# A transformer layer on one Trainium2 core: value norms moved into the output weights, four attention output buffers, spread normalisations and no paired units

## The reference

```python
def _L0_attn_ref(x, wq, wk, wv, wo, q_norm_w, k_norm_w):
    xq = _rms_norm(x @ wq.T, q_norm_w, EPS)      # 32 heads of 64
    xk = _rms_norm(x @ wk.T, k_norm_w, EPS)      # 8 heads of 64
    xv = x @ wv.T
    ...
    allowed = (dist <= 0) & (dist >= -SLIDING_WINDOW)     # 256
    bias = jnp.where(allowed[None], alibi, -jnp.inf)
    scores = jnp.einsum('bhtd,bhsd->bhts', xq, xk) * scale + bias[None]
    attn = jax.nn.softmax(scores, axis=-1)
    out = jnp.einsum('bhts,bhsd->bhtd', attn, xv)
    out = out.transpose(0, 2, 1, 3).reshape(bsz, seqlen, N_HEADS * HEAD_DIM)
    return out @ wo.T
...
x = x + _layernorm(_L0_attn_ref(_layernorm(x), ...))
x = x + _layernorm(_L0_ffn_ref(_layernorm(x), ...))   # silu(x Wg * gs) * (x Wu * us) Wd * ds, 1408 wide
```

## Time and profile before

| | |
|---|---|
| median of 3 runs | 1206.97 us (1206.37 to 1208.41) |
| the profiled execution | 1207.18 us, span 1205.0 us |
| granted TensorE clock, mean | 0.994 |
| PE busy | 1164.7 us (97% of the span) |
| DVE busy | 891.2 us (74%) |
| ACT busy | 745.9 us (62%) |
| POOL busy | 392.1 us (33%) |

### The profile page before, as it was taken

One profiled execution on the slowest core, in us unless ns is written; L12 is line 12 of the kernel. 1 busy time (PEld: TensorE's weight loads), 2 busy tenths in 40 slices (PEclk: granted clock), 3 DMA queues, 4 the chain that ended last, 5 costly groups with the idle time before them and its releaser, 6 DMA issues.

```text
span 1205.0 us, 26933 instructions
## 1 busy us (share of the span) xinstructions
PE 1164.7 (97%) x9016; PEld 994.3 (83%) x9016; DVE 891.2 (74%) x2328; ACT 745.9 (62%) x1582; POOL 392.1 (33%) x465
## 2 busy tenths in 40 slices
PE   7999999999888899999999999999999999999997
PEld 5878888887777788898989898898888888888876
DVE  5587778687888878888888888888866575546464
ACT  4646555555888778888878888788862443222230
POOL 3000000001799865354544545354531100202022
PEclk9999999999999999999999999999999999999999
DMA  5216355347667774556545664556437440303020
GB/s 175 105 45 245 141 212 206 140 193 261 215 232 246 245 252 137 184 164 220 158 152 178 205 203 139 179 171 217 128 95 237 146 130 30 105 1 106 1 70 36
DMA packets 100132, 189.89 MB, mean 158 GB/s; under 512 B 8352, under 2 KB 38176, under 8 KB 100000
## 3 DMA queue, kind: packets, MB, share of 16 engines
q1 hardware_dynamic: 100000, 188.21, 46.3%
HBM read 116.54 MB, written 71.63 MB: 156 GB/s over the span
## 4 chain that ended last, share of the span: by engine, by line
PE 88%; POOL 5%; DVE 3%; issue 2%; ACT 1%; DMA 1%; SPq 0%; POOLq 0%; DVEq 0%; ACTq 0%
PE bank L1384 21%; PE bank L1517 19%; PE bank L1449 15%; PE bank L1322 11%; PE bank L1410 10%; PE bank L1428 2%; PE bank L1438 2%; PE bank L1426 2%; PE bank L1427 2%; POOL qk L697 1%; POOL bias L663 1%; POOL o_mid L672 1%; DMA q_st<-q_scr 1%; POOL o_out L678 1%; PE bank L1494 1%
## 5 line engine op out<-in xcount | busy, mean ns | idle before, releaser
L781 ACT ACTIVATE p_sb<-u_sb,low 128x384 f32<-128x384 f32 (+2 forms) x512 | 272.5, 536 | 49.4 <-DVE low L1030 40.8
L1030 DVE CUSTOM_DVE_ANT_0 u_sb<-bank,bias 128x384 f32<-128x384 f32 (+2 forms) x512 | 229.8, 452 | 50.8 <-PE bank L1322 28.2
L1322 PE MATMUL bank<-k_st,q_st 128*128 128x384 f32 (+2 forms) x1024 | 254.7, 331 | 1.9 <-DMA q_st<-q_scr 1.4
L1410 PE MATMUL bank<-ident,p_sb 128*128 128x128 f32 x1152 | 218.3, 280 | 21.0 <-ACT p_sb L781 13.7
L1144 DVE TENSOR_TENSOR pT_lo<-bank,pT_hi 128x384 f16<-128x384 f32 (+2 forms) x392 | 178.5, 455 | 34.5 <-ACT pT_hi L889 27.4
L889 ACT ACTIVATE pT_hi<-bank 128x384 f16<-128x384 f32 (+2 forms) x392 | 159.9, 408 | 42.9 <-PE bank L1410 38.3
L1322 PEld LDWEIGHTS bank<-k_st,q_st 128*128 128x128 f32 x1024 | 170.5, 193 | 18.9 <-DMA q_st<-q_scr 1.7
L1410 PEld LDWEIGHTS bank<-ident,p_sb 128*128 128x128 f32 x1152 | 141.1, 141 | 51.3 <-ACT p_sb L781 27.9
L672 POOL TENSOR_TENSOR o_mid<-o_raw,inv_sum 128x256 f32<-128x256 f32 x128 | 83.8, 654 | 227.8 <-DVE inv_sum L1156 226.3
L634 POOL TENSOR_TENSOR rstd<-var_eps,minus_half 128x1 f32<-128x1 f32 (+1 forms) x30 | 22.6, 752 | 413.8 <-DVE var_eps L999 413.8
L1517 PE MATMUL bank<-zT_hi,gu 128*128 128x512 f32 x352 | 139.3, 396 | 0.6 <-DVE hid L1273 0.6
(11 more groups left out here) (128 smaller groups left out, 2396.1 us busy)
## 6 DMA issues: line engine op xcount, KB each, us to landing
q_scr<-qk SPq DMA_DIRECT2D x64, 512.0 KB, 2.7
q_st<-q_scr SPq DMA_DIRECT2D x32, 1024.0 KB, 7.8
k_st<-k_scr SPq DMA_DIRECT2D x64, 256.0 KB, 3.2
o_scr<-o_out SPq DMA_DIRECT2D x128, 128.0 KB, 2.9
o_in<-o_scr SPq DMA_DIRECT2D x16, 768.0 KB, 5.2
k_scr<-qk SPq DMA_DIRECT2D x16, 512.0 KB, 2.6
z_in<-z_scr SPq DMA_DIRECT2D x8, 1024.0 KB, 5.9
v_scr<-v_out SPq DMA_DIRECT2D x4, 1040.0 KB, 6.6
```

The source lines that it names most:

```text
L781: nc.scalar.activation(p_sb[:, u % RING, 0:w], u_sb[:, u % RING, 0:w], ACT.Exp, scale=-1.0, bias=low[:, u % RING:u % RING + 1]).then_inc(p ...
L1030: nc.vector.tensor_tensor_reduce(out=u_sb[:, u % RING, 0:w], in0=bank[u % 2][:, 0:w], in1=bias[2 * u // UNITS][:, u % REP, at:at + w], sca ...
L1322: mm = nc.tensor.matmul(bank[u % 2][:, 0:w], q_st[:, s, r, P * i:P * i + P], k_st[:, s, part, P * key:P * key + w], start=(part == 0), sto ...
L1410: mm = nc.tensor.transpose(bank[probability_bank(A)][:, P * j:P * j + P], p_sb[:, u % RING, P * j:P * j + P], ident[:])
```

## The change

- The norms of the values go into wo: `split_wo` first multiplies a chunk of wo by `vn_col`, which holds the norms of two heads as a column (row d of wo belongs to value dimension d), then rounds and subtracts as before. `vn_col` is loaded from one row of `vn_scr` by two transfers of 512 elements of 4 bytes. `finish_o` is one multiplication.
- `o_raw` and `inv_sum` have four buffers (`O_RING`), released by `o_ready`.
- Late normalisations: four in group 0, three in groups 1 and 2, none in 3, and one each in groups 4 to 10, at unit 8. The last seven chunks (f = 13 to 19) have memory of their own (`raw_last`) and one buffer of their own (`qk_late`). SP checks the ring's stores in group 3 (`rings_stored`).
- TWINS = 0: each unit is rounded and split by itself from the start, by `LAGS`, through banks 2 and 3.

```diff
-TWINS = LAG * UNITS - 2 * TT
+TWINS = 0
 RING = 4
+O_RING = TT
...
-LATE_UNITS = (2, 4, 18, 20, 22)
+LATE_COUNTS = {0: 4, 1: 3, 2: 3, **{n: 1 for n in range(LAG, LAG + 7)}}
+LATE_AT = {4: (2, 4, 18, 20), 3: (4, 18, 20), 1: (8,)}
 LATE_NORMS = {}
-for _k, _f in enumerate(range(LATE, QC + KVC)):
-    LATE_NORMS[_k // len(LATE_UNITS), LATE_UNITS[_k % len(LATE_UNITS)]] = _f
+for _n, _count in LATE_COUNTS.items():
+    for _u in LATE_AT[_count]:
+        LATE_NORMS[_n, _u] = LATE + len(LATE_NORMS)
+LATE_OWN = LATE + sum(_count for _n, _count in LATE_COUNTS.items() if _n < LAG)
...
-            inv_sum = sb(s2, "inv_sum", [P, 2, REP])
-            sb(s2, "spare", [P, REP * HD])
-            o_raw = sb(s2, "o_raw", [P, 2, REP, O_COLS])
-            o_mid = sb(s2, "o_mid", [P, REP, HD])
+            inv_sum = sb(s2, "inv_sum", [P, O_RING, REP])
+            o_raw = sb(s2, "o_raw", [P, O_RING, REP, O_COLS])
...
+        def own(b, f):
+
+            return isinstance(b, int) and b == B - 1 and f >= LATE_OWN
+
+        def qk_buffer(b, f):
+
+            return qk_late if own(b, f) else qk[:, f % QK_RING]
...
+            def rings_stored():
+
+                for s in range(QK_RING):
+                    sp.wait_ge(qk_stored[s], qk_stores(B - 1, 0) + DMA * len(range(s, LATE_OWN, QK_RING)))
+                sp.wait_ge(v_stored, DMA * B)
...
-            sp.dma_start(v_norm[:, 0:G].rearrange("p g d -> p (g d)"), vn_scr).then_inc(vn_loaded, DMA)
-            sp.dma_start(v_norm[:, G:G + 2].rearrange("p g d -> p (g d)"), vn_scr[:, 0:2 * HD]).then_inc(vn_loaded, DMA)
+            for half in range(2):
+                sp.dma_start(vn_col[HD * half:HD * half + HD, :], vn_scr[0].rearrange("(g d) -> d g", g=G),
+                             allow_slow_non_contiguous=True).then_inc(vn_loaded, DMA)
...
                 pool.wait_ge(inv_sum_ready, a + 1)
-                at_least(pool, o_ready, a)
-                nc.gpsimd.tensor_tensor(out=o_mid[:], in0=o_raw[:, i % 2, :, 0:HD],
-                                        in1=inv_sum[:, i % 2].unsqueeze(2).broadcast_to([P, REP, HD]),
-                                        op=ALU.mult).then_inc(o_mid_ready, 1)
-                pool.wait_ge(o_mid_ready, a + 1)
                 at_least(pool, o_stored[i], DMA * (2 * n + s))
                 hold(pool)
-                nc.gpsimd.tensor_tensor(out=o_out[:, i], in0=o_mid[:],
-                                        in1=v_norm[:, 2 * (n % TT) + s:2 * (n % TT) + s + 1].broadcast_to([P, REP, HD]),
+                nc.gpsimd.tensor_tensor(out=o_out[:, i], in0=o_raw[:, i, :, 0:HD],
+                                        in1=inv_sum[:, i].unsqueeze(2).broadcast_to([P, REP, HD]),
                                         op=ALU.mult).then_inc(o_ready, 1)
...
+                chunk = TT * group + i
+                g = 2 * chunk // REP
                 pool.wait_ge(wo_loaded, DMA * (group + 1))
...
+                nc.gpsimd.tensor_tensor(out=wo_stage[:, i], in0=wo_stage[:, i], in1=vn_col[:, g:g + 1].broadcast_to([P, D]),
+                                        op=ALU.mult).then_inc(wo_scaled, 1)
+                pool.wait_ge(wo_scaled, chunk + 1)
+                nc.gpsimd.tensor_copy(wo_hi[:, chunk], wo_stage[:, i]).then_inc(wo_hi_ready, 1)
...
-                at_least(act, o_mid_ready, a - 1)
-                nc.scalar.activation(o_raw[:, u // REP % 2].rearrange("p r d -> p (r d)"),
+                at_least(act, o_ready, a - O_RING + 1)
+                nc.scalar.activation(o_raw[:, u // REP % O_RING].rearrange("p r d -> p (r d)"),
...
                 if A < TWINS:
                     at_least(pe, pT_ready, A - A % 2 - 2)
                 else:
-                    at_least(pe, pT_ready, A - 1 if A > TWINS + 1 else TWINS - 2)
+                    at_least(pe, pT_ready, A - 1)
```

More of the change, by code:

```diff
@@ L126, in feed_forward_slots @@
     return slots
-LATE_UNITS = (2, 4, 18, 20, 22)
+LATE_COUNTS = {0: 4, 1: 3, 2: 3, **{n: 1 for n in range(LAG, LAG + 7)}}
+LATE_AT = {4: (2, 4, 18, 20), 3: (4, 18, 20), 1: (8,)}
 LATE_NORMS = {}
-for _k, _f in enumerate(range(LATE, QC + KVC)):
-    LATE_NORMS[_k // len(LATE_UNITS), LATE_UNITS[_k % len(LATE_UNITS)]] = _f
+for _n, _count in LATE_COUNTS.items():
+    for _u in LATE_AT[_count]:
+        LATE_NORMS[_n, _u] = LATE + len(LATE_NORMS)
+LATE_OWN = LATE + sum(_count for _n, _count in LATE_COUNTS.items() if _n < LAG)
 def late_norms(n, first, end):
-    return [LATE_NORMS[n, u] for u in LATE_UNITS if first <= u < end and (n, u) in LATE_NORMS]
+    return [LATE_NORMS[n, u] for u in range(first, end) if (n, u) in LATE_NORMS]
 SLOTS = feed_forward_slots()
@@ L261, in sandwich_layer @@
             norm_w = sb(s1, "norm_w", [P, QC + KVC])
-            with ExitStack() as before_norms:
-                w_stage = sb(before_norms, "w_stage", [P, 2, KC, T])
-            qk = sb(s1, "qk", [P, QK_RING, 2, T], F32R)
+            inv_rms = sb(s1, "inv_rms", [P, 2, T])
+            raw_last = sb(s1, "raw_last", [P, QC + KVC - LATE_OWN, T])
+            raw = [raw_first[:, f] if f < LATE_OWN else raw_last[:, f - LATE_OWN] for f in range(QC + KVC)]
         with ExitStack() as s2:
@@ L274, in sandwich_layer @@
             y_raw = sb(s2, "y_raw", [P, D])
-            sb(s2, "spare4", [P, REP * WIN - D])
-            v_norm = sb(s2, "v_norm", [P, G + 2, HD])
+            qk_late = sb(s2, "qk_late", [P, 2, T], F32R)
+            vn_col = sb(s2, "vn_col", [P, G])
+            sb(s2, "spare5", [P, (G + 2) * HD - G])
             f_bits = sb(s2, "f_bits", [P, PARTS, D])
@@ L444, in store_qk @@
                 sp.dma_start(scr[bass.ds(head, 2)].rearrange("h d t n -> (h d) t n"),
[L445 removed]
+                             qk_buffer(b, f)[:].bitcast(F32)).then_inc(qk_late_stored if own(b, f) else qk_stored[f % QK_RING], DMA)
             def stage1_stored(batches):
@@ L812, in square_v @@
                 for kc in range(KC):
-                    nc.scalar.activation(raw[:, QC + kc], w_stage[:, 1, kc], ACT.Square).then_inc(v_squared, 1)
+                    nc.scalar.activation(raw[QC + kc], w_stage[:, 1, kc], ACT.Square).then_inc(v_squared, 1)
             def norm_of_v():
                 act.wait_ge(v_norm_psum, 1)
-                nc.scalar.activation(raw[:, QC + KVC - 1], bank[7][:], ACT.Sqrt, scale=VSCALE ** -2,
+                nc.scalar.activation(raw[QC + KVC - 1], bank[7][:], ACT.Sqrt, scale=VSCALE ** -2,
                                      bias=eps_tiny[:]).then_inc(v_norm_ready, 1)
@@ L822, in round_raw @@
                 act.wait_ge(scaled, (QC + KVC) * b + f + 1)
-                at_least(act, qk_stored[f % QK_RING], qk_stores(b, f))
-                nc.scalar.activation(qk[:, f % QK_RING, 0], raw[:, f], ACT.Copy).then_inc(qk_hi_ready, 1)
+                if own(b, f):
+                    at_least(act, qk_late_stored, DMA * (f - LATE_OWN))
+                else:
+                    at_least(act, qk_stored[f % QK_RING], qk_stores(b, f))
+                nc.scalar.activation(qk_buffer(b, f)[:, 0], raw[f], ACT.Copy).then_inc(qk_hi_ready, 1)
             def project(b, last=False):
@@ L851, in project @@
                         at_least(act, qk_ready, (QC + KVC) * (b - 1) + n + 1)
-                        nc.scalar.activation(raw[:, n], bank[n % 4][:], ACT.Copy).then_inc(raw_ready, 1)
+                        nc.scalar.activation(raw[n], bank[n % 4][:], ACT.Copy).then_inc(raw_ready, 1)
                         if n in (0, QC):
@@ L1356, in project @@
                             pe.wait_ge(v_squared, kc + 1)
-                            mm = nc.tensor.matmul(bank[7][:], ones[:], raw[:, QC + kc], start=(kc == 0), stop=(kc == KC - 1))
+                            mm = nc.tensor.matmul(bank[7][:], ones[:], raw[QC + kc], start=(kc == 0), stop=(kc == KC - 1))
                         mm.then_inc(v_norm_psum, 1)
```

39 lines of the change are left out of this document (19 added, 20 removed).

## The result

The changed kernel takes 1216.68 us (median of 4 runs, 1214.99 to 1217.69), the kernel before beside it 1207.69 (median of 4). The ratio is 1.0074, its 95% interval 1.0061 to 1.0087. So it is slower, by 0.7%, as forecast (1210.1), but by 9.0 us instead of 2.9, and 0.7 us above the end of the range. The profiled execution took 1217.23 us with a span of 1215.5, from the first to the last instruction.

What follows compares the result with a forecast made beforehand. PE was taken to bound the attention from group 4 on (99% busy), POOL's stalls to slow groups 0 to 3. Groups 0 to 3 -9.3, unit 8 of groups 4 to 10 +12.2: +2.9 on 1207.2 gives 1210.1 us, range 1201 to 1216.

Steps and rivals of the forecast that it cites:

- (a): Groups 0 to 3: POOL's shorter work and four o_raw buffers remove the stalls, -10.9 us.
- (b): Groups 0 to 3: seven of 17 late normalisations leave, -2.8 us; the ten that stay cost +0.2 each, +2.0.
- the rule: Groups 0 to 3 without stalls: 7.7 us a heavy quarter, 7.1 a light one, 0.4 a late normalisation, 125.9 in all.
- (c): Groups 0 to 3, couples dissolved: heavy quarters +9.6 us, light quarters -7.2, net +2.4.
- Its chain: Single units on ACT and DVE: round, split, add_bias, exp, round; 2.09 us for two units, plus 0.26 for o_raw's copy.
- (e): Groups 4 to 10, unit 8: DVE's scaling waits for POOL's bias, PE stalls; 1.75 us seven times, +12.2.
- (f): Groups 11 to 15, projections and feed forward: only POOL's finish_o gets shorter, 0 us.
- Rival A: Groups 4 to 10: the scaling meets no bias, so unit 8 costs 3.5 us; 1201.4 us, chance 0.33.
- C: Rival, groups 1 to 3: POOL still ends last, only 5 us of stalls go; 1216.0 us, chance 0.09.
- B: Rival, groups 0 to 3: single units take 1.17 us each, light quarters gain nothing; 13.6 us, 1221.3 total, chance 0.10.
- The prediction's own sign of being wrong: Scalings of 0.75 us at unit 8 with groups of 39.3 us, or groups 0 to 3 above 131 us together.

Runs made afterwards that it cites:

- e4: The changed kernel with units below 120 coupled again as in the kernel before; groups 0 to 3 together took 123.7 us.
- e12: The changed kernel with single units below 120 at the couples' lags through four PSUM banks, seven late normalisations at unit 12; 1194.15 us, ratio 0.9889 to before.
- e1: The changed kernel with POOL making only 16 of 384 bias columns for units 16 to 31 in groups 4 to 10; 1209.11 us.
- e2: The changed kernel with the seven late normalisations of groups 4 to 10 at unit 12 instead of 8; 1205.81 us.
- e11: The changed kernel with the seven scalings at unit 8 cut to 16 of 512 columns, POOL's bias whole; groups took 40.3 us.
- e7: The changed kernel with DVE's split four units behind instead of three and weighing five behind, below unit 120; groups 0 to 3 took 160.3 us.
- e8: The kernel before with only the couples dissolved (TWINS = 0); groups 0 to 3 together took 138.6 us.

## Why the prediction was right in sign and too small

- **(a) and (b), stalls and moved normalisations: right.** -10.9 - 2.8 = -13.7 was said; with couples kept, e4 measures 123.7 - 136.8 = -13.2. Some luck is in this: in e4 the eight heavy quarters took 64.5 us where the rule has 61.6, because the last of group 3 takes 9.9 and not 7.7, and the light ones with their ten normalisations and the start 59.1 where it has 61.5. POOL's busy time, 26.4 us in group 1, came below the 28.8 said, of which 1.6 were waits.
- **(c), couples: the step that failed.** +2.4 was said; +4.4 with the +2.0 for the ten that stay, which the prediction has in (b), for POOL's third wo operation. Measured was +9.5 for both. What failed is the gain of the light quarters in single units, and the price of a late normalisation there. Its chain stands: heavy quarters take 8.64 us (8.9 said), and in the kernel after the chain reads as foretold. ACT and DVE of group 1, the units 10 to 13, against the earlier trace rows:

```profile
340.36 0.56 DVE L1168 TENSOR_TENSOR pT_lo<-bank,pT_hi 128x384 f16<-128x384 f32 x1
...
341.43 0.62 ACT L802 ACTIVATE p_sb<-u_sb,low 128x384 f32<-128x384 f32 x1 [0.15 <-DVE low L1054]
341.95 0.37 ACT L925 ACTIVATE o_raw<-bank 128x260 f32<-128x260 f32 x1
342.21 0.48 ACT L913 ACTIVATE pT_hi<-bank 128x384 f16<-128x384 f32 x1
...
342.73 0.56 DVE L1168 TENSOR_TENSOR pT_lo<-bank,pT_hi 128x384 f16<-128x384 f32 x1 [0.20 <-ACT pT_hi L913]
```

  From split to split of one parity 2.37 us with the copy of o_raw in it, where the prediction has 2.09 + 0.26. By its terms, from the starts of the exponentials in e4 and in the kernel after: heavy quarters, said +9.6, measured +6.0 (seven are 0.6 to 1.4 dearer, the last of group 3 is 0.4 cheaper). Light quarters, said -7.2, measured 8 x (6.63 - 6.84) = -1.7: I took 6.2 from a quarter of group 7, where a unit has 1.1 us and the chain is slack, and 7.07, the coupled one, still had 0.2 in it that e4 hasn't. Remaining normalisations, said +2.0, measured +5.2, what is left of the 9.5. One reason was foreseen, the scalings held by POOL (five of them by 0.4 us, so up to 2 us). The other wasn't: DVE's scaling and ACT's copy come into a chain that has little room for them, and I had priced them by what they cost where two units shared an instruction. With the other lags of e12, where no scaling lasts over 0.80 us, one still costs 0.7, (7.60 - 6.2) / 2. How the 5.2 us divide between the two no run tells.
- **(e), the collision: right in mechanism, 1.5 us short.** Said: bias 552.0 to 554.8 beside unit 8, scaling to 0.55 behind it, DVE 1.75 us late, 1.75 us a group, 12.2 in all. Measured: a scaling of 1.82 us that holds DVE for 1.75 (557.00 to 558.75), 2.0 a group, 13.7 in all. Only its parts were mis-sized: I gave 0.65 to a normalisation without collision (0.5 and 0.15 by e), e1 gives 0.97; the bias adds 1.05, not 1.1.
- **(f): right within 0.6 us** of 193.2 for groups 11 to 15.
- Rival A, no collision, is refuted by the seven scalings of 1.73 to 1.83 us. Had the seven stood at unit 12, the same working would have given A's 1201.4; e2 took 1205.81, so (c) would have missed there too. C is refuted by POOL's 79%. B's chain of 1.17 us a unit is refuted by heavy quarters of 8.64 (1.08 a unit), but its other half, no gain in light quarters, was nearly what came. The prediction's own sign of being wrong, groups 0 to 3 above 131 us, came as well (133.1).
- By the profiles the sum was 10.5 us, 1.4 of them ahead of the attention; by the medians 9.0. Against the forecast (c) with the +2.0 gave 5.1 more, (e) 1.5, (a) and (b) 0.5, and groups 11 to 15 with what follows 0.9 less: 2.9 + 6.2 = 9.1.

## What to carry to other kernels

Before a VectorE instruction with two operands in SBUF is moved, look up on POOL's time line what runs at the new place: a collision costs what is left of POOL's instruction, even for a moved one of sixteen columns (e11), and costs it on the path if the stretch has no slack. And a construct that comes as a bundle (two units an instruction, other lags, more banks) should be taken apart before it is judged: here the lags with the banks were worth 11 us, and the four groups were 1.8 us shorter without the pairing. A chain is read by writing down which instruction stands ahead of which on each engine, and counting how many units one round of it advances.

## What the runs showed of the hardware

- The exclusion is of whole instructions and of their start. A scaling of 16 columns, issued 1.27 us ahead of the end of POOL's 2.74 us bias, lasted 1.30 us; the split of oT with one operand in PSUM ran in 0.69 us beside the same bias, as long as without it. That agrees with the Trainium skill, page "SBUF — State Buffer", section "Who interferes with whom", and holds here for an instruction of 2.74 us, which the prediction had left open.
- It works both ways and between short instructions too: in groups 0 to 2 of the kernel after scalings begun beside the wo multiplication lasted 1.12 to 1.15 us instead of 0.75, and POOL's copy of wo, begun at 348.69 beside such a scaling (348.02 to 349.17), lasted 0.95 us where its median is 0.61.
- The granted clock fell in some stretches where PE waited much, and not in others. In e7 it went from 1.00 to 0.50, so from 2.4 to 1.2 GHz, at about 356.2 us, in a pause of PE from 355.20 to 356.43 behind a heavy quarter with PE busy 8.4 of 9.95 us, and the light quarter, 0.63 on average, took 11.8 us where the kernel after took 8.3 at 1.00. In group 3 of the same run PE was busy 8.26 of 9.93 us, its longest pause in the light quarter that followed was 0.59 us, and the clock stayed at 1.00 (8.13 us); in e8 it stayed there through a pause of 1.69 us. No run shows what decides it, nor how much of the 3.5 us is clock.
